# A graph layer's hot-edge counts stored column first, then source block, instead of block first

## The chip, the cores and the metric

One core of a Trainium2 chip runs the whole layer. The metric is the device time of the kernel in microseconds. The trace is one profiled execution of the same program.

## What is computed

A graph layer with three attention heads on 6,250 nodes of 128 features and 100,000 edges sorted by their target `dst`, followed by a layer norm. Cut to what matters:

```python
a_k  = exp(relu(concat(h[src], h[dst]) @ W_att_k + b_att_k))           # k = 1, 2, 3, one number per edge
att_k = segment_sum(a_k, dst)
msg  = relu(relu(relu(h[src] @ W_msg_1 + b) @ W_msg_2 + b) @ W_msg_3 + b)
m    = (a_1/att_1[dst] + a_2/att_2[dst] + a_3/att_3[dst]) / 3 * msg
out  = relu(concat(h, segment_sum(m, dst)/max(deg, 1)) @ W_c1 + b) @ W_c2 + b
x    = layernorm(x + out)
```

The message and the two halves of the attention logit depend on a node alone, so they are computed once per node. The targets are drawn unevenly: the low node numbers receive many more edges than the high ones.

## The kernel before

**Table.** A first phase computes for every node its message row and its three logits and stores them in DRAM as `message_table`. Nodes are cut into 49 blocks of 128.

**Edges by gather.** Edges are taken in groups of 256, two tiles of 128. For groups 94 to 390 (297 of them) GpSimd fetches the 128 message rows of each tile with one indirect DMA (L1154), 594 in all, into a ring of eight places of four tiles. Units are walked in order, one unit per step of all engines' loops: unit 0 has two groups, units 1 to 23 have four and take two places of the ring, units 24 to 125 have two and take one. GpSimd may fill a place once TensorE's sums of the unit that used it before are done (`s_sum`); for unit 86 that is unit 78, for unit 23 it is unit 19. In each step VectorE sums the parts of the target's logit (L1634), adds the logit of the gathered rows (L1638), waits for ScalarE's exponential (L1404), clips it (L1646) and makes weights (L1651). TensorE multiplies rows by weights (L1281) and sums the weights (L1285), and VectorE adds the result to `acc` (L1668). L1592 makes one-hot vectors for units to come.

**Hot edges by counting.** The first 94 groups point at the first 384 nodes. Their edges are not gathered but counted. A group's targets lie in a window of `w` nodes (6, 9 or 10 by the place of the group). For each edge, a number in `comb_t` joins the source's block number and the target's place in the window; targets outside the window get 4096 added so that they match nothing. VectorE turns it into a one-hot row of 49 `w` columns by comparison with a running index (`one_hots`, L1526), ScalarE makes a one-hot row of the source's place within its block (L1418, L1423), and TensorE multiplies both (L1302): the result, in a PSUM bank, is the number of edges for each place, block and column of the window. VectorE adds it to `counts` at the window's start (`add_counts`, L1539), four groups a step, in steps 1 to 24. The table `counts` holds, per partition (the source's place in its block), 49 blocks times 384 hot nodes as 16-bit integers.

**The dense product.** From step 26 on, one source block a step and 49 blocks in all: for each head ScalarE adds logits (L1374) and takes the exponential into a single PSUM bank (L1383). VectorE clips it and multiplies it by the counts of this block (`hot_weights`, L1561, three a step, 147 in all) into `hot_wt`, and TensorE multiplies `hot_wt` by the block's message rows (L1319). ScalarE may write the bank again when the weighting that reads it is done, and the weighting waits for its exponential. In a step's order on VectorE stand: head 0's weighting, L1634, L1638, L1646, L1651, head 1's weighting, L1592, head 2's weighting, L1668 twice.

After it come the final stages per group of node blocks (L836 and on, L927 and on), spread over the remaining steps, and a layer norm.

Of the kernel before, what the change touches and what calls it, by code (L numbers as in the profile page):

```python
# [45 lines left out]
CELL = 32  # L46
SUMS_AT = 64
FLT_MAX = 3.4028234663852886e38
# [42 lines left out]
def gnn_program(nc, x, x_t, src, dst, w_first, w_rest, b_rows, table, hot_table, near_table, q_table, out, n_edges):  # L91
    f32, bf16, i32 = mybir.dt.float32, mybir.dt.bfloat16, mybir.dt.int32
    ALU, ACT, AX = mybir.AluOpType, mybir.ActivationFunctionType, mybir.AxisListType.X

    n_nodes = x.shape[0]
    n_blocks = -(-n_nodes // P)
# [8 lines left out]
    n_hot = HOT_GROUPS  # L105
# [8 lines left out]
    def width_of(g):  # L114

        if g < n_hot:
            return HOT_WIDTHS[g // CELL]
        share = min(1.0, (g // CELL + 1) * CELL / n_groups)
        mean = 2 * GROUP * n_nodes / n_edges * share
        return min(WIN, 4 * -(-int(mean + 12 * share + 2 + 3.99) // 4))  # L120
# [17 lines left out]
    def block_nodes(i):  # L138
        return min(P, n_nodes - i * P)
# [5 lines left out]
    with ctx:  # L145
        def sb(name, shape, dt=f32):
            return ctx.enter_context(nc.sbuf_tensor(name, shape, dt))

        def sem(name):
            return ctx.enter_context(nc.semaphore(name))  # L150


        counts_flat = sb("counts", [P, hot_nodes * n_blocks], u16)
        counts = counts_flat[:, :].rearrange("p (b d) -> p b d", b=n_blocks)
        logits_or_x = sb("logits_or_x", [P, max(HEADS * hot_nodes, TWO * COLS)])
        hot_ld = logits_or_x[:, 0:HEADS * hot_nodes].rearrange("p (k d) -> p k d", k=HEADS)
        x_cols = logits_or_x[:, 0:TWO * COLS].rearrange("p (j n) -> p j n", j=TWO)
# [61 lines left out]
        comb_t = fin[:, at_index:at_index + n_hot * TILES].rearrange("p (g h) -> p g h", h=TILES)  # L219
# [21 lines left out]
        dst_t = sb("dst_t", [P, n_hot, TILES], bf16)  # L241
# [115 lines left out]
        def chained(eng, s):  # L357

            count = [0]

            def chain(instruction):
                count[0] += 1
                instruction.then_inc(s, 1)
                eng.wait_ge(s, count[0])
            return chain
# [239 lines left out]
        LEFT_BANK = COUNT_BANKS[LEFT_NEXT % FOUR]  # L605
        hot_end = HOT_AT + n_blocks + 2
        HOT_ADDED = 3
        INDEX_STEPS = 5 + len(range(0, n_hot, CELL))
        edges = [0, CELL, SUMS_AT, n_hot]
        assert HOT_WIDTHS[0] <= HOT_WIDTHS[1] <= HOT_WIDTHS[2] and SUMS_AT == 2 * CELL  # L610
        tally_parts = [(slice(0, n_hot), d) for d in range(HOT_WIDTHS[0])]
# [98 lines left out]
        s_cadd = sem("s_cadd")  # L710
# [5 lines left out]
        s_hw = sem("s_hw")  # L716
# [300 lines left out]
        def edge_pass(first):  # L1017
# [123 lines left out]
            with Straight(nc) if first else nc.Block() as block:  # L1141
# [221 lines left out]
                def _(act):  # L1363
# [42 lines left out]
                    def low_hots(step):  # L1406

                        if step == 0:
                            act.wait_ge(s_ix, INDEX_STEPS)
                            act.wait_ge(s_nt1, 16)  # L1410
# [63 lines left out]
                def _(dve):  # L1474
# [23 lines left out]
                    if first:  # L1498
                        index = chained(dve, s_ix)
                        scratch = hit[:, 0:2, 0:n_hot * TILES].bitcast(i32)  # L1500
                        low, high = (scratch[:, j, :].rearrange("p (h g) -> p h g", h=TILES) for j in range(2))
                        beyond = hit[:, 2, 0:n_hot * TILES].rearrange("p (g h) -> p g h", h=TILES)
                        of_src = src_t[:, :, 0:n_hot]
                        dve.wait_ge(s_src, 16)
                        index(dve.tensor_scalar(low, of_src, P - 1, None, ALU.bitwise_and))
                        index(dve.tensor_scalar(high, of_src, 7, None, ALU.logical_shift_right))
                        index(dve.tensor_copy(lo_t[:, :, :], low.rearrange("p h g -> p g h")))
                        index(dve.tensor_copy(comb_t[:, :, :], high.rearrange("p h g -> p g h")))
                        for g in range(0, n_hot, CELL):
                            cell, w = slice(g, min(g + CELL, n_hot)), float(width_of(g))  # L1510
                            dve.tensor_scalar(beyond[:, cell, :], dst_t[:, cell, :], w, BEYOND, ALU.is_ge, ALU.mult)
                            index(dve.scalar_tensor_tensor(comb_t[:, cell, :], comb_t[:, cell, :], w,
                                                           dst_t[:, cell, :], ALU.mult, ALU.add))
                        index(dve.tensor_tensor(comb_t[:, :, :], comb_t[:, :, :], beyond, ALU.add))

                    hot_window = window_registers(dve, n_hot, lambda g: hot_nodes - width_of(g))
# [12 lines left out]
                    def add_counts(step):  # L1529
                        if step == 0:  # L1530
                            dve.wait_ge(s_zero, zeroed)
                        for g in range(step * PAIRS, min((step + 1) * PAIRS, n_hot)):
                            w = width_of(g)
                            start = hot_window(g)
                            dve.wait_ge(s_ct, (g + 1) * TILES)
                            if g >= 1:
                                dve.wait_ge(s_cadd, g)
                            here = counts[:, :, bass.ds(start, w)]
                            dve.tensor_tensor(here, here, bank[COUNT_BANKS[g % FOUR]][:, 0:w * n_blocks].rearrange(  # L1539
                                "p (b d) -> p b d", d=w), ALU.add).then_inc(s_cadd, 1)  # L1540

                    def tally_hot():

# [12 lines left out]
                    def hot_weights(b, k):  # L1556
                        m, n = block_nodes(b), HEADS * b + k
                        dve.wait_ge(s_he, n + 1)
                        if b >= THREE:
                            dve.wait_ge(s_hm, b - THREE + 1)  # L1560
                        dve.scalar_tensor_tensor(hot_wt[0:m, b % THREE, k, :], bank[EXP_BANK][0:m, 0:hot_nodes],  # L1561
                                                 FLT_MAX, counts[0:m, b, :], ALU.min, ALU.mult).then_inc(s_hw, 1)

                    def copy_hot():

# [110 lines left out]
                    for i in range(n_steps):  # L1676
                        hot_step = first and 0 <= i - HOT_AT - 1 < n_blocks
                        if hot_step:
                            hot_weights(i - HOT_AT - 1, 0)
                        if i + 1 < n_units:  # L1680
                            logits_of(i + 1)
                        if first and 0 <= i - 1 < COUNT_STEPS:
                            add_counts(i - 1)
# [4 lines left out]
                        if hot_step:  # L1688
                            hot_weights(i - HOT_AT - 1, 1)
                        if i + AHEAD < n_units and by_dve(i + AHEAD):  # L1690
                            one_hot(i + AHEAD)
                        if hot_step:
                            hot_weights(i - HOT_AT - 1, 2)
# [129 lines left out]
```

## Time and profile before

| what | value |
|---|---|
| time, median of 3 runs (lowest, highest) | 826.16 us (826.0, 827.2) |
| the profiled execution, its own time | 826.97 us |
| its span, first to last instruction | 822.9 us |
| mean granted TensorE clock | 0.809 of full |
| GpSimd busy | 590.9 us, 72% |
| TensorE matmul busy | 656.1 us, 80% |
| VectorE busy | 577.4 us, 70% |
| ScalarE busy | 381.7 us, 46% |

Busy is time in which an instruction of the engine ran; issuing and waiting don't count. The span leaves out some 4 us around the first and last instruction. PE is TensorE, DVE VectorE, ACT ScalarE, POOL GpSimd.

### The profile page before, as it was taken

To read this page: it belongs to the slowest core of one execution; us is meant where nothing else is said; L and a number is where in the kernel's file an instruction comes from. 1 tells how busy PE (TensorE), PEld (TensorE's weight loads), DVE (VectorE), ACT (ScalarE), POOL (GpSimd) and SP (SyncE) were. 2 spreads that over 40 slices of the span, in tenths; PEclk is the share of its full clock that TensorE was granted. 3 is DMA by queue.
4 is the path that set the end of the run, shared out by engine and by line. 5 is a ranking of instruction groups with operands and counts; after the bars stand their busy time and mean duration, and the time that the engine had idled before them with its cause. 6 is when DMAs were issued, how large, how long until landed. Compare 5 with 4: busy or idle time off the path is not lost.

```text
span 822.9 us, 16893 instructions
## 1 busy us (share of the span) xinstructions
PE 656.1 (80%) x4917; PEld 512.9 (62%) x4917; DVE 577.4 (70%) x1934; ACT 381.7 (46%) x999; POOL 590.9 (72%) x638
## 2 busy tenths in 40 slices
PE   9945677777578778989898988888877978878885
PEld 5734455544345446778787877776666766667664
DVE  4882656585688877677776767775577868787766
ACT  5522555463444443677676767662123322333323
POOL 7437777777777777777777777777777777777770
PEclk9975555567565675799999999999699989998989
DMA  6533222225652233333333333334233443443421
GB/s 190 142 105 69 63 65 65 65 65 57 71 65 62 62 92 78 74 87 76 80 82 75 83 78 84 77 77 131 65 90 102 112 108 102 104 130 101 98 58 35
DMA packets 79474, 70.44 MB, mean 86 GB/s; under 512 B 34040, under 2 KB 65312, under 8 KB 79376
## 3 DMA queue, kind: packets, MB, share of 16 engines
q0 software_dynamic: 19008, 39.88, 22.2%
q1 hardware_dynamic: 60080, 29.28, 13.3%
q8 instruction: 42, 0.69, 0.3%
q14 instruction: 56, 0.46, 0.2%
q10 hardware_dynamic: 288, 0.13, 0.1%
HBM read 62.32 MB, written 6.90 MB: 84 GB/s over the span
## 4 chain that ended last, share of the span: by engine, by line
POOL 35%; DVE 21%; issue 19%; PE 17%; ACT 4%; DMA 2%; DVEq 2%; ACTq 0%; SPq 0%; POOLq 0%
POOL work L1154 34%; DVE fin L1561 4%; PE bank L1281 4%; DVE acc L1668 3%; ACT bank L1383 3%; DVE counts L1539 2%; DVE fin L1526 2%; DVE fin L927 2%; PE bank L836 2%; PE bank L565 2%; PE bank L544 2%; DMA work<-message_table,src_t 1%; PE bank L1285 1%; PE bank L1319 1%; DVE side L1592 1%
## 5 line engine op out<-in xcount | busy, mean ns | idle before, releaser
L1154 POOL DMA_INDIRECT work<-message_table,src_t x594 | 566.4, 953 | 191.8 <-issue 178.0
L1281 PE MATMUL bank<-work 128*128 128x144 f32 (+8 forms) x1188 | 248.7, 343 | 66.5 <-DVE acc L1668 66.4
L1281 PEld LDWEIGHTS bank<-work 128*128 128x128 f32 x1188 | 197.7, 234 | 100.4 <-issue 86.0
L1444 ACT COPY work<-bank 128x192 f32<-128x192 f32 (+7 forms) x126 | 37.4, 297 | 250.9 <-DVE work L1634 246.5
L1319 PE MATMUL bank<-work,fin 128*128 128x129 f32 (+1 forms) x882 | 117.3, 290 | 0.0
L1668 DVE TENSOR_TENSOR acc<-acc,bank 128x192 f32 (+8 forms) x297 | 88.7, 299 | 31.3 <-issue 7.5
L1319 PEld LDWEIGHTS bank<-work,fin 128*128 128x128 f32 (+1 forms) x882 | 108.2, 201 | 2.5 <-issue 0.6
L1383 ACT ACTIVATE bank<-hot_logit 128x384 f32<-128x384 f32 (+1 forms) x147 | 72.7, 494 | 70.9 <-DVE fin L1561 62.0
L1651 DVE TENSOR_TENSOR work<-bank,work 128x576 f32<-128x576 f32 (+7 forms) x126 | 86.2, 684 | 13.1
L1285 PE MATMUL bank<-work 128*4 128x48 f32 (+8 forms) x1188 | 95.0, 207 | 0.0
L1561 DVE SCALAR_TENSOR_TENSOR fin<-bank,counts 128x384 f32<-128x384 f32 (+1 forms) x147 | 81.4, 554 | 18.1 <-ACT bank L1383 17.4
L1302 PE MATMUL bank<-fin 128*128 128x294 bf16 (+2 forms) x188 | 63.7, 506 | 35.6 <-DVE fin L1526 20.4
L1374 ACT ACTIVATE hot_logit<-logits_or_x,work 128x384 f32<-128x384 f32 (+1 forms) x147 | 88.3, 600 | 0.0
L1638 DVE TENSOR_TENSOR work<-work 128x12 f32<-128x12 f32 (+1 forms) x126 | 22.2, 176 | 80.5 <-DMA work<-message_table,src_t 70.6
L836 PE MATMUL bank<-rest_w,acc 128*128 128x128 f32 x294 | 48.0, 324 | 34.2 <-DVE fin L927 29.3
L1285 PEld LDWEIGHTS bank<-work 128*4 128x4 f32 x1188 | 50.0, 88 | 38.3 <-issue 8.5
L1539 DVE TENSOR_TENSOR counts<-counts,bank 128x294 f32 (+2 forms) x94 | 57.4, 611 | 22.4 <-DVE counts L1539 12.8
L836 PEld LDWEIGHTS bank<-rest_w,acc 128*128 128x128 f32 x294 | 42.4, 227 | 36.5 <-DVE fin L927 30.6
L1302 PEld LDWEIGHTS bank<-fin 128*128 128x128 bf16 x188 | 22.5, 125 | 63.6 <-ACT fin L1423 30.7
L1418 ACT ACTIVATE fin<-fin 128x128 bf16<-128x128 f16 x188 | 59.3, 386 | 1.2 <-PE bank L1302 1.2
L1404 ACT ACTIVATE work<-work 128x12 f32<-128x12 f32 (+1 forms) x126 | 26.8, 213 | 65.4 <-DVE work L1638 63.7
L1646 DVE TENSOR_SCALAR work<-work 128x12 f32<-128x12 f32 (+1 forms) x126 | 24.5, 194 | 41.7 <-ACT work L1404 40.4
(132 smaller groups left out, 688.9 us busy)
## 6 DMA issues: line engine op xcount, KB each, us to landing
work<-message_table,src_t POOLq DMA_INDIRECT x594
side<-near_nodes SPq DMA_DIRECT2D x102, 48.0 KB
side<-logit_parts SPq DMA_DIRECT2D x297, 0.8 KB
message_table<-work SPq DMA_DIRECT2D x12, 262.0 KB, 3.4
work<-message_table SPq DMA_DIRECT2D x48, 65.5 KB
work<-in_x_t SPq DMA_DIRECT2D x12, 256.0 KB, 3.3
fin<-in_x SPq DMA_DIRECT2D x11, 256.0 KB, 2.9
logits_or_x<-in_x_t SPq DMA_DIRECT2D x11, 256.0 KB
```

Of the source, the lines that this page charges most:

```text
L836: last = pe.matmul(to[:, k * P:(k + 1) * P], acc[:, k, nodes], wc1[:, 1, :], start=True, stop=True)
L1154: pool.indirect_dma_start(out=rows_of(n)[:, t, :], out_offset=None, in_=table[:, :], in_offset=bass.IndirectOffsetOnAxis(ap=src_t[:, h, g: ...
L1281: pe.matmul(sums[:, at:at + HEADS * w], rows_here[:, t, 0:P], wt_of(i)[:, t, :], start=h == 0, stop=h == TILES - 1)
L1285: last = pe.matmul(sums[SUMS_AT:SUMS_AT + HEADS + 1, at + HEADS * w:at + HEADS * w + w], a_col[:, i % THREE, t, :], mask_of(i)[:, t, :], s ...
L1302: pe.matmul(bank[COUNT_BANKS[g % FOUR]][:, 0:n], hot_lo[:, t % HOT_RING, :], hot_comb[:, t % HOT_RING, 0:n], start=h == 0, stop=h == TILES ...
L1319: last = pe.matmul(bank[SIDE_BANKS[h]][:, k * (P + 1):(k + 1) * (P + 1)], hot_wt[0:m, b % THREE, k, h * P:(h + 1) * P], rows_here, start=F ...
L1374: act.activation(hot_logit[0:m, n % TWO, :], hot_ld[0:m, k, :], ACT.Relu, bias=hot_block[0:m, b % BLOCKS, 1 + P + k:2 + P + k]).then_inc(s ...
L1383: act.activation(bank[EXP_BANK][0:m, 0:hot_nodes], hot_logit[0:m, n % TWO, :], ACT.Exp).then_inc(s_he, 1)
L1539: dve.tensor_tensor(here, here, bank[COUNT_BANKS[g % FOUR]][:, 0:w * n_blocks].rearrange("p (b d) -> p b d", d=w), ALU.add).then_inc(s_cad ...
L1561: dve.scalar_tensor_tensor(hot_wt[0:m, b % THREE, k, :], bank[EXP_BANK][0:m, 0:hot_nodes], FLT_MAX, counts[0:m, b, :], ALU.min, ALU.mult). ...
L1651: dve.tensor_tensor(wt_of(i).rearrange("p t (k w) -> p t k w", w=w), from_q(i)[:, :, PARTS:PARTS + w].unsqueeze(2).to_broadcast([P, n, HEA ...
L1668: dve.tensor_tensor(here, here, sums[:, at:at + (HEADS + 1) * w].rearrange("p (k w) -> p k w", w=w), ALU.add).then_inc(s_acc, 1)
```

## The change

The table of counts and the columns of a group's product change their order from block first, then node, to node first, then block. The addition's operand becomes one run of 49 `w` elements of `counts`, since all blocks of one node now lie side by side. The dense product's weighting reads one block's 384 counts at a step of 49 elements. The joined number becomes 49 times the place in the window plus the block number, so that one multiply-add over all groups takes the place of three by width. The comparison with the window's width stays.

```diff
-        counts = counts_flat[:, :].rearrange("p (b d) -> p b d", b=n_blocks)
+        counts = counts_flat[:, :].rearrange("p (d b) -> p d b", b=n_blocks)
...
-        INDEX_STEPS = 5 + len(range(0, n_hot, CELL))
+        INDEX_STEPS = 6
...
                             dve.tensor_scalar(beyond[:, cell, :], dst_t[:, cell, :], w, BEYOND, ALU.is_ge, ALU.mult)
-                            index(dve.scalar_tensor_tensor(comb_t[:, cell, :], comb_t[:, cell, :], w,
-                                                           dst_t[:, cell, :], ALU.mult, ALU.add))
+                        index(dve.scalar_tensor_tensor(comb_t[:, :, :], dst_t[:, :, :], float(n_blocks),
+                                                       comb_t[:, :, :], ALU.mult, ALU.add))
                         index(dve.tensor_tensor(comb_t[:, :, :], comb_t[:, :, :], beyond, ALU.add))
...
-                            here = counts[:, :, bass.ds(start, w)]
+                            here = counts[:, bass.ds(start, w), :]
                             dve.tensor_tensor(here, here, bank[COUNT_BANKS[g % FOUR]][:, 0:w * n_blocks].rearrange(
-                                "p (b d) -> p b d", d=w), ALU.add).then_inc(s_cadd, 1)
+                                "p (d b) -> p d b", d=w), ALU.add).then_inc(s_cadd, 1)
...
                         dve.scalar_tensor_tensor(hot_wt[0:m, b % THREE, k, :], bank[EXP_BANK][0:m, 0:hot_nodes],
-                                                 FLT_MAX, counts[0:m, b, :], ALU.min, ALU.mult).then_inc(s_hw, 1)
+                                                 FLT_MAX, counts[0:m, :, b], ALU.min, ALU.mult).then_inc(s_hw, 1)
```

## Rows read from the trace of the kernel before

**Rows 1.** The page's costliest groups: busy us, mean ns, idle before, releaser.

```profile
L1154 POOL DMA_INDIRECT work<-message_table,src_t x594 | 566.4, 953 | 191.8 <-issue 178.0
```

**Rows 2.** View of L1154 (ns min/median/max, first and last start), then GpSimd's waits.

```profile
L1154 POOL DMA_INDIRECT work<-message_table,src_t x594: 940/944/1833, 54.2 to 800.4; - x198
...
POOL work L1154 <- PE bank L1285: 2.4, 8, 0.3
```

**Rows 3.** Timeline of two places of the ring: start us, us, instruction, idle before.

```profile
275.56 0.35 PE L1285 MATMUL bank<-work 128*4 128x28 f32 x4
...
281.87 0.95 POOL L1154 DMA_INDIRECT work<-message_table,src_t  x1 [0.30 <-issue]
...
580.00 0.35 PE L1285 MATMUL bank<-work 128*4 128x44 f32 x4
...
602.32 0.94 POOL L1154 DMA_INDIRECT work<-message_table,src_t  x1 [0.30 <-PE bank L1285]
```

**Rows 4.** Timeline, TensorE's last sums of units 29, 58 and 77.

```profile
341.01 0.28 PE L1285 MATMUL bank<-work 128*4 128x32 f32 x4
...
475.37 0.31 PE L1285 MATMUL bank<-work 128*4 128x40 f32 x4
...
569.13 0.32 PE L1285 MATMUL bank<-work 128*4 128x44 f32 x4
```

**Rows 5.** Timeline of VectorE, one step of the dense product.

```profile
396.95 0.56 DVE L1561 SCALAR_TENSOR_TENSOR fin<-bank,counts 128x384 f32<-128x384 f32 x1
...
398.44 0.17 DVE L1646 TENSOR_SCALAR work<-work 128x12 f32<-128x12 f32 x1 [0.55 <-ACT work L1404]
398.72 0.61 DVE L1651 TENSOR_TENSOR work<-bank,work 128x432 f32<-128x432 f32 x1
399.24 0.55 DVE L1561 SCALAR_TENSOR_TENSOR fin<-bank,counts 128x384 f32<-128x384 f32 x1
...
400.41 0.56 DVE L1561 SCALAR_TENSOR_TENSOR fin<-bank,counts 128x384 f32<-128x384 f32 x1 [0.37 <-ACT bank L1383]
400.89 0.70 DVE L1668 TENSOR_TENSOR acc<-acc,bank 128x128 f32 x2
401.59 0.56 DVE L1561 SCALAR_TENSOR_TENSOR fin<-bank,counts 128x384 f32<-128x384 f32 x1
```

**Rows 6.** View of L1638 in 341 to 570 us, then 565 to 823: idle us, times.

```profile
  DMA work<-message_table,src_t: 4.6, 6
...
  DMA work<-message_table,src_t: 22.0, 14
```

**Rows 7.** VectorE's groups by shape: busy us, mean ns, idle before.

```profile
L1561 DVE SCALAR_TENSOR_TENSOR fin<-bank,counts 128x384 f32<-128x384 f32 x144 | 79.8, 554 | 17.7 <-ACT bank L1383 17.1 <-PE bank L1319 0.4
...
L1539 DVE TENSOR_TENSOR counts<-counts,bank 128x490 f32 x30 | 20.6, 686 | 7.8 <-DVE counts L1539 3.8 <-issue 2.9 <-PE bank L1302 0.9
...
L1539 DVE TENSOR_TENSOR counts<-counts,bank 128x441 f32 x32 | 20.1, 627 | 7.2 <-DVE counts L1539 4.2 <-issue 2.9
...
L1539 DVE TENSOR_TENSOR counts<-counts,bank 128x294 f32 x32 | 16.8, 524 | 7.4 <-DVE counts L1539 4.8 <-issue 2.5
```

**Rows 8.** View of L1539 (ns min/median/max), then two neighbours in its timeline.

```profile
L1539 DVE TENSOR_TENSOR counts<-counts,bank x94: 460/617/815, 83.6 to 316.5; 128x294 f32 x32, 128x441 f32 x32, 128x490 f32 x30
...
113.09 0.46 DVE L1539 TENSOR_TENSOR counts<-counts,bank 128x294 f32 x1 [0.20 <-DVE counts L1539]
113.75 0.60 DVE L1539 TENSOR_TENSOR counts<-counts,bank 128x294 f32 x1 [0.20 <-DVE counts L1539]
```

**Rows 9.** Timeline of VectorE, three of the index preparations.

```profile
55.46 0.26 DVE L1505 TENSOR_SCALAR logits_or_x<-src_t 128x188 int32<-128x188 int32 x1
...
56.04 0.26 DVE L1507 CAST fin<-logits_or_x 128x188 f32<-128x188 int32 x1
...
57.92 0.35 DVE L1514 TENSOR_TENSOR fin<-fin,logits_or_x 128x188 f32<-128x188 f32 x1
```

**Rows 10.** Stretches: us, PE, PEld, DVE, ACT, POOL busy, clock, DMA share, GB/s.

```profile
250.00:320.00 70.00, 53.05 (x323) 33.36 (x324) 58.05 (x162) 27.51 (x78) 52.94 (x57) 0.62 0.29 73
345.00:475.70 130.70, 118.35 (x1072) 104.69 (x1069) 92.95 (x276) 93.03 (x222) 98.80 (x105) 0.96 0.34 81
```

## The prediction

> **What bounds the kernel now.** I read the costliest groups first. One group stands out: GpSimd issues 594 indirect gathers of message rows (L1154), each 0.95 us, and nearly all of its 191.8 us of idle time between them is issue time [rows 1]. The line's own view gives the first at 54.2 us and the last at 800.4 us: (800.4 - 54.2) / 593 = 1.258 us each, and in the list of waits the only other releaser inside that stream is the edge sums of TensorE (L1285), 2.4 us in 8 pieces of at most 0.3 us, no longer than the issue gap itself [rows 2]. So from 54 us to 800 us GpSimd never stops. The span is 54.2 + 746.2 + a tail of 22.5 us behind the last gather's start, and nothing that VectorE saves in between can move the end; only what makes GpSimd wait, or leaves VectorE and TensorE with a backlog behind the last gather, can.
>
> GpSimd may run eight ring places ahead of the edge sums. I read from the timeline how near it came to that limit. In the counting stage the place for the gathers starting at 281.87 us was free when the sum of four long units before had ended at 275.56 + 0.35 = 275.91: 6.0 us of slack, the least of the whole run. The gather at 602.32 us is the 437th, the first of unit 86; it needs the sum of unit 78, which ended at 580.00 + 0.35: 22.0 us of slack [rows 3]. Unit 78 is the first behind the dense product, whose 49 blocks ride on steps 27 to 76.
>
> In the dense stage the edge sums of unit 29 end at 341.29, those of unit 58 at 475.68, and those of unit 77 at 569.45 us [rows 4]: 228.2 us for 48 steps, 4.75 us a step, against 4 x 1.258 = 5.03 us for a unit's gathers. The stage is a little faster than the gathers and eats backlog. What sets a step is seen in VectorE's timeline, one step from 396.95 to 401.59 us [rows 5]. All three weightings (L1561) stand in VectorE's order; idle are 0.55 us for ScalarE's exponential of the edges and 0.37 us for the next hot exponential in PSUM (one bank, so ScalarE waits for each weighting in turn). Those idle times follow from ScalarE's own work behind the previous weighting and don't shrink if a weighting grows. So a weighting longer by x lengthens the step by 3x.
>
> How much of such a delay is swallowed? VectorE's first addition that needs gathered rows (L1638) waited for the gather DMA 4.6 us in the dense stage and 22.0 us from there to the end [rows 6]. A consumer that is late doesn't wait there. So 26.6 us of lateness disappear. The ring says the same in another way: after 4.6 us swallowed in the stage, 22.0 us of slack before GpSimd must stop.
>
> **The change part by part.** (1) Addition of counts, 94 times. It took 524, 627 and 686 ns as means of its three widths, 57.5 us in all [rows 7]. Its minimum is 460 ns, and neighbours of the same 294 elements took 0.46 and 0.60 us [rows 8]; what differs is the node at which the window starts, hence where the 49 short runs of 12 bytes lie. I take the one-run form at the good value of each width: 460 for 294 elements, and by VectorE's slope of (554 - 460) / (384 - 294) = 1.04 ns per element [rows 7, 8] 613 for 441 and 664 for 490. Saved: 32 x 64 + 32 x 14 + 30 x 22 ns = 3.2 us of VectorE. Up to about 225 us VectorE waits for gathers anyway and the slack of the ring is never used up, so this saves nothing at the end; of the wider groups some 0.8 us reach the start of the dense stage as less backlog. If the window start multiplied by 49 needs one more register step of some tens of ns each, this vanishes too.
>
> (2) Indices. Three chained multiply-adds become one over 188 elements; the addition behind it has that size and took 0.35 us [rows 9]. That stands near 57 us, before the first gathered rows are used, and the gain of some 0.4 us is hidden by the gathers. Comparisons, one-hots, matmuls and their sizes are unchanged: a group's 49 w columns are only in another order.
>
> (3) The dense product's weighting, 147 times, now reads its 384 counts at a step of 49 elements, 98 bytes, instead of as one run. Today 554 ns [rows 7]. This is the price that decides, and no row shows this very access. Lower bound: L1507 reads int32 at a step of 376 bytes and took 0.26 us, as L1505 does over the same 188 elements read in a row [rows 9], so x = 0. But that instruction alternates between two runs, so each neighbour comes back two elements later, while a step of 98 bytes never comes back. Upper bound: a badly placed window of 49 short runs costs 0.60 - 0.46 = 0.14 us more, 2.9 ns per jump [rows 8]; 384 jumps would be x = 1.1 us. Nearer to the new access is the mean over placements, since 98-byte steps run through all of them: 524 - 460 = 64 ns for 49 jumps, 1.3 ns per jump, read and write together [rows 7, 8]. If the read alone pays all of it, x = 384 x 1.3 = 0.50 us; if it pays half, 0.25 us. I take 0.40 us, about one more cycle per element by the slope above, so a weighting of 0.95 us. A rule of the Trainium skill speaks against this change: "Vector Engine (DVE) Microarchitecture Reference", section "Measured stream behaviour on trn2", holds that a port keeps its rate only over adjacent pairs of words, and gives 1.73 ns an element for a source that hops every time and 2.50 ns for steps of 24 words, against 1.054 ns. By it, as an estimate, x would be 0.26 or 0.56 us, on both sides of mine; no row of this trace shows such a step, and by the row of L1507 alone x would be nothing.
>
> (4) The sum. Lateness made: 49 x 3 x 0.40 = 58.8 us, less 0.8 us from (1). Swallowed: 26.6 us. Left: 58.8 - 0.8 - 26.6 = +31.4 us. GpSimd's issue is then stretched by the same 31 us, mostly between about 400 and 650 us, when the ring is full. In general the end moves by 147 x - 27.4 us once x is over 0.186 us, and not at all below. The profiled execution took 826.97 us at a span of 822.9; the median of the runs is 826.16. 826.16 + 31.4 = 857.6 us; I say 857.5.
>
> **Rivals.** What a measurement of this kernel can tell from no change is 0.2%, 1.7 us.
>
> A, the forecast, weighting between 0.85 and 1.15 us: +17 to +60 us. Chance 0.47.
>
> B, a mild price, x between 0.19 and 0.30 us: +1 to +17 us; 0.25 gives +9.4, 835.5 us. For it: half of the mean jump price, and a source in PSUM that may hide part. Chance 0.20, of which 0.02 lies within 0.2%.
>
> C, the other side: the strided read is free or nearly so. The place is the read in L1561, the point is x = 0.186 us. GpSimd stays unbroken and the time is 826.2 us; the 3.2 us of the additions show on VectorE and nowhere at the end. For it: L1507, and most windows whose runs jump 768 bytes at no price; against it: those runs still hold 6 or more elements per jump. Chance 0.18, including 0.03 for a gain over 0.2% by less contention at the tail.
>
> D, heavier: x over 0.60 us (at the upper bound 147 x 1.1 - 27.4 = +134 us), or TensorE's clock falls in the dense stage. It was granted 0.62 in 250 to 320 us and 0.96 in 345 to 475.7 us, where TensorE was busy 118.35 of 130.7 us, 4.2 us a step [rows 10]; at a step of 5.95 us it would be busy 71%. At half clock its work would be at most 8.1 us a step (4.23 x 0.96 / 0.5), longer than VectorE's, and the end 49 x (8.1 - 4.65) - 27 = +142 us if it held for the whole stage. Against it: from 345 us on it kept the upper of its two levels, 2.4 GHz, nearly all the time, at shares of 80% and more. Chance 0.15.
>
> So slower by over 0.2%: 0.47 + 0.18 + 0.15 = 0.80; within 0.2%: 0.02 + 0.15 = 0.17; faster 0.03. The range has to include C and nearly all of A: 825 to 885 us (x from 0 to 0.58). It leaves out D and little else.
>
> **What the profile of the changed kernel would show.** L1561 near 0.95 us instead of 0.55; the addition at L1539 near 460, 613 and 664 ns with hardly any spread; steps in the dense stage of about 5.9 us; waits of GpSimd's L1154 for TensorE's L1285 of some 30 us, from the middle of the dense stage on; L1638 hardly waiting for gathers after it; the first gather still at 54 us and the tail behind the last one near 22 us. The prediction is wrong if L1561 stays under 0.74 us, if ScalarE's exponentials turn out to leave slack that hides part of 3x, or if the clock falls.

## The result and the profile after

The changed kernel takes 867.16 us (median of 4 runs, 864.21 to 869.08) against 826.46 us for the one before (4 runs): 40.7 us more. The ratio on record is 1.0508, interval 1.0490 to 1.0526; it is formed from the single runs and not from these two medians, whose own ratio is 1.0492. The profiled execution took 866.57 us at a span of 862.5 us, 39.6 us more than the span of before.

VectorE's groups by shape in the changed kernel (busy us, mean ns, idle before), the lines that answer to [rows 7]:

```profile
L1561 DVE SCALAR_TENSOR_TENSOR fin<-bank,counts 128x384 f32<-128x384 f32 x144 | 140.8, 978 | 16.9 <-ACT bank L1383 16.9
...
L1539 DVE TENSOR_TENSOR counts<-counts,bank 128x490 f32 x30 | 20.0, 667 | 8.6 <-DVE counts L1539 4.8 <-issue 2.6 <-PE bank L1302 0.9
L1539 DVE TENSOR_TENSOR counts<-counts,bank 128x441 f32 x32 | 19.7, 616 | 8.0 <-DVE counts L1539 4.8 <-issue 3.0
```

The weighting went from 554 to 978 ns, so x is 0.424 us, and 147 of them make 62.3 us. The additions took what one run should: 667 and 616 ns here, and the view of the line gives the minimum as before and the maximum down from 815 to 671 ns. In sum they fell from 57.4 to 54.5 us:

```profile
L1539 DVEq FUSED_REGOPS  x94: 57/64/71, 83.3 to 317.0; - x94
L1539 DVE TENSOR_TENSOR counts<-counts,bank x94: 460/615/671, 83.5 to 317.1; 128x294 f32 x32, 128x441 f32 x32, 128x490 f32 x30
```

The register step in front of each addition now takes 64 ns at the median; it was 46. The idle time of VectorE before the additions grew from 22.4 to 24.4 us over all 94, so VectorE gained 0.9 us and not 2.9.

One step on VectorE's timeline, answering to [rows 5]:

```profile
396.72 0.98 DVE L1561 SCALAR_TENSOR_TENSOR fin<-bank,counts 128x384 f32<-128x384 f32 x1
...
398.62 0.22 DVE L1646 TENSOR_SCALAR work<-work 128x12 f32<-128x12 f32 x1 [0.54 <-PE bank L1285]
398.94 0.56 DVE L1651 TENSOR_TENSOR work<-bank,work 128x384 f32<-128x384 f32 x1
399.42 0.97 DVE L1561 SCALAR_TENSOR_TENSOR fin<-bank,counts 128x384 f32<-128x384 f32 x1
...
401.01 0.98 DVE L1561 SCALAR_TENSOR_TENSOR fin<-bank,counts 128x384 f32<-128x384 f32 x1 [0.36 <-ACT bank L1383]
401.91 0.70 DVE L1668 TENSOR_TENSOR acc<-acc,bank 128x128 f32 x2
402.61 0.98 DVE L1561 SCALAR_TENSOR_TENSOR fin<-bank,counts 128x384 f32<-128x384 f32 x1
```

The step lasts 5.89 us, 1.25 more than the 4.64 of before, which is 3 x 0.42; the two idle pieces are the same (0.54 and 0.36 against 0.55 and 0.37). The profile puts this 0.54 us down to TensorE's L1285; most of the waits before L1646, 36.5 of 43.4 us on the page, it puts down to ScalarE's L1404 as before. Over the whole stage the steps grew by 1.24 us: 287.5 / 48 = 5.99 us against 4.75. TensorE's last sums of units 29 and 77, and of the last unit, 125:

```profile
341.96 0.28 PE L1285 MATMUL bank<-work 128*4 128x32 f32 x4
...
629.42 0.32 PE L1285 MATMUL bank<-work 128*4 128x44 f32 x4
...
847.86 0.33 PE L1285 MATMUL bank<-work 128*4 128x48 f32 x4
```

Against [rows 4] unit 29 is 0.9 us later, unit 77 60.3 us later (629.74 - 569.45), the last one (808.77 us before) 39.4 us later. So the delay is made in the dense stage, and a third of it vanishes behind it. (Some 2 us of the 60.3 arise at unit 77 itself, by a lower clock there; see "3x per step" below.) GpSimd's own view and its waits, answering to [rows 2]:

```profile
L1154 POOL DMA_INDIRECT work<-message_table,src_t x594: 938/944/1754, 54.3 to 832.9; - x198
```

```profile
POOL work L1154 <- issue: 166.5, 546, 0.4
POOL work L1154 <- PE bank L1285: 48.8, 45, 2.8
```

It is held 45 times, 48.8 us with the issue gaps of 0.3 us in them, some 35 us without. The first time shows on its timeline at 441.79 us, and from there to 636 us the ring is full:

```profile
441.79 0.94 POOL L1154 DMA_INDIRECT work<-message_table,src_t  x1 [1.01 <-PE bank L1285]
...
636.07 0.94 POOL L1154 DMA_INDIRECT work<-message_table,src_t  x1 [1.36 <-PE bank L1285]
```

The second row is unit 86's first gather, 33.8 us later than in [rows 3]; it is the last one that is held. The last gather starts at 832.9 us, 29.6 us before the end of the span, where it was 22.5 us. From the dense stage on L1638 no longer waits for gathers: in 341 us to the end its views show no such wait, where [rows 6] had 4.6 and 22.0 us.

### The profile page after: what moved, and what is told of

It reads as the page before. It is cut to its first block, busy times and chain, and to the rows that moved or that the text cites. A ratio compares the mean times of both kernels' runs of the same rounds, so it can differ in the third digit from the quotient of the medians.

```text
span 862.5 us, 16891 instructions
## 1 busy us (share of the span) xinstructions
PE 665.2 (77%) x4917; PEld 521.0 (60%) x4917; DVE 637.5 (74%) x1932; ACT 381.4 (44%) x999; POOL 588.2 (68%) x638
## 3 DMA queue, kind: packets, MB, share of 16 engines
q1 hardware_dynamic: 60080, 29.28, 12.7%
## 4 chain that ended last, share of the span: by engine, by line
DVE 36%; issue 18%; PE 18%; POOL 15%; ACT 8%; DVEq 2%; DMA 2%; ACTq 0%; SPq 0%; POOLq 0%
POOL work L1154 15%; DVE fin L1561 14%; PE bank L1281 5%; ACT bank L1383 5%; DVE acc L1668 4%; DVE counts L1539 2%; DVE fin L927 2%; PE bank L836 2%; DVE fin L1526 2%; DVE work L1646 2%; PE bank L1285 2%; DVE side L1592 2%; PE bank L544 2%; DVE work L1651 1%; PE bank L565 1%
## 5 line engine op out<-in xcount | busy, mean ns | idle before, releaser
L1154 POOL DMA_INDIRECT work<-message_table,src_t x594 | 563.7, 949 | 226.8 <-issue 166.5
L1281 PEld LDWEIGHTS bank<-work 128*128 128x128 f32 x1188 | 195.5, 232 | 139.7 <-issue 126.5
L1561 DVE SCALAR_TENSOR_TENSOR fin<-bank,counts 128x384 f32<-128x384 f32 (+1 forms) x147 | 143.8, 978 | 17.3 <-ACT bank L1383 17.2
L1444 ACT COPY work<-bank 128x192 f32<-128x192 f32 (+7 forms) x126 | 37.4, 297 | 247.7 <-DVE work L1634 246.8
L1319 PE MATMUL bank<-work,fin 128*128 128x129 f32 (+1 forms) x882 | 129.4, 309 | 0.0
L1319 PEld LDWEIGHTS bank<-work,fin 128*128 128x128 f32 (+1 forms) x882 | 119.8, 219 | 2.4 <-issue 0.2
L1285 PE MATMUL bank<-work 128*4 128x48 f32 (+8 forms) x1188 | 94.9, 207 | 0.0
L1302 PE MATMUL bank<-fin 128*128 128x294 bf16 (+2 forms) x188 | 64.5, 513 | 37.4 <-DVE fin L1526 26.6
L1285 PEld LDWEIGHTS bank<-work 128*4 128x4 f32 x1188 | 49.9, 88 | 38.0 <-issue 8.2
L1539 DVE TENSOR_TENSOR counts<-counts,bank 128x294 f32 (+2 forms) x94 | 54.5, 580 | 24.4 <-DVE counts L1539 14.8
L836 PE MATMUL bank<-rest_w,acc 128*128 128x128 f32 x294 | 46.1, 315 | 26.2 <-DVE fin L927 25.4
L1638 DVE TENSOR_TENSOR work<-work 128x12 f32<-128x12 f32 (+1 forms) x126 | 21.9, 174 | 58.6 <-DMA work<-message_table,src_t 46.4
L1302 PEld LDWEIGHTS bank<-fin 128*128 128x128 bf16 x188 | 22.5, 128 | 66.3 <-ACT fin L1423 34.9
L1418 ACT ACTIVATE fin<-fin 128x128 bf16<-128x128 f16 x188 | 59.3, 386 | 1.2 <-PE bank L1302 1.2
L836 PEld LDWEIGHTS bank<-rest_w,acc 128*128 128x128 f32 x294 | 40.8, 220 | 28.4 <-DVE fin L927 26.6
L1646 DVE TENSOR_SCALAR work<-work 128x12 f32<-128x12 f32 (+1 forms) x126 | 24.0, 191 | 43.4 <-ACT work L1404 36.5
L1592 DVE TENSOR_SCALAR side<-side,less_col 48x512 bf16<-48x512 bf16 x149 | 52.6, 366 | 0.0
```

What stands on the lines that cost most here:

```text
L836: last = pe.matmul(to[:, k * P:(k + 1) * P], acc[:, k, nodes], wc1[:, 1, :], start=True, stop=True)
L1154: pool.indirect_dma_start(out=rows_of(n)[:, t, :], out_offset=None, in_=table[:, :], in_offset=bass.IndirectOffsetOnAxis(ap=src_t[:, h, g: ...
L1281: pe.matmul(sums[:, at:at + HEADS * w], rows_here[:, t, 0:P], wt_of(i)[:, t, :], start=h == 0, stop=h == TILES - 1)
L1285: last = pe.matmul(sums[SUMS_AT:SUMS_AT + HEADS + 1, at + HEADS * w:at + HEADS * w + w], a_col[:, i % THREE, t, :], mask_of(i)[:, t, :], s ...
L1302: pe.matmul(bank[COUNT_BANKS[g % FOUR]][:, 0:n], hot_lo[:, t % HOT_RING, :], hot_comb[:, t % HOT_RING, 0:n], start=h == 0, stop=h == TILES ...
L1319: last = pe.matmul(bank[SIDE_BANKS[h]][:, k * (P + 1):(k + 1) * (P + 1)], hot_wt[0:m, b % THREE, k, h * P:(h + 1) * P], rows_here, start=F ...
```

## Experiments

**Which part of the change makes the time.** The changed kernel with a contiguous read:

```diff
-                                                 FLT_MAX, counts[0:m, :, b], ALU.min, ALU.mult).then_inc(s_hw, 1)
+                                                 FLT_MAX, counts_flat[0:m, b * hot_nodes:(b + 1) * hot_nodes], ALU.min, ALU.mult).then_inc(s_hw, 1)
```

> The changed kernel, but the weighting reads 384 counts in one run (the counts it reads belong to other nodes and blocks, so the dense product is not the layer's). Theory, the strided read alone sets the change: L1561 back at 554 ns, GpSimd issues without a stop from 54 to 800 us, time 826.5 us, within 1.7. The additions stay at 460, 615 and 667 ns and their 3 us do not show at the end. Rival 1, the rest of the change (longer register step of 57 to 71 ns in place of 46 before each of 94 additions, other index arithmetic) costs what my sum missed: 829 to 832 us. Rival 2, the faster additions reach the end: 823 to 824.5 us.

Measured: 826.91 us against 826.62 before, ratio 1.0006 (0.9996 to 1.0015). Its shapes:

```profile
L1561 DVE SCALAR_TENSOR_TENSOR fin<-bank,counts 128x384 f32<-128x384 f32 x144 | 79.8, 554 | 17.3 <-ACT bank L1383 17.3
...
L1539 DVE TENSOR_TENSOR counts<-counts,bank 128x294 f32 x32 | 14.8, 463 | 7.9 <-DVE counts L1539 5.1 <-issue 2.6
```

The faster additions (463 ns in place of 524 for the narrow groups), with their longer register step, and the single index step are worth nothing at the end. Both rivals fall.

The other half, the kernel before with the strided read alone:

```diff
+        by_node = counts_flat[:, :].rearrange("p (d b) -> p d b", b=n_blocks)
...
-                                                 FLT_MAX, counts[0:m, b, :], ALU.min, ALU.mult).then_inc(s_hw, 1)
+                                                 FLT_MAX, by_node[0:m, :, b], ALU.min, ALU.mult).then_inc(s_hw, 1)
```

> The kernel before, its additions and indices as they were; only the weighting reads at a step of 49 elements (the counts it reads belong to other nodes and blocks, so the dense product is not the layer's). Theory: L1561 near 978 ns, step of the dense stage 5.9 to 6.0 us, GpSimd held by the edge sums for 30 to 35 us, time 864 to 869 us as for the whole change. Rival 1, of the 40.7 us some 5 come from the rest of the change: 860 to 863 us.

Measured: 866.56 us, ratio 1.0474 (1.0440 to 1.0509). The view of the line (one number later here, for the added line):

```profile
L1562 DVE SCALAR_TENSOR_TENSOR fin<-bank,counts x147: 953/978/1017, 326.4 to 619.1; 128x384 f32<-128x384 f32 x144, 106x384 f32<-106x384 f32 x3
```

The strided read alone loses 39.9 us (36 to 42 by the interval), against 40.7 for the whole change; the rival of 860 to 863 us falls, narrowly. GpSimd was held 48.8 us in 41 pieces, some 36.5 without issue gaps, a little over the 30 to 35 expected. One kernel with everything but the strided read loses nothing, the other with the strided read alone loses all: this pair settles the cause.

**Is a first part of the lateness free?** The same kernel with `by_node[0:m, :, b] if k < 1 else counts[0:m, b, :]`, so that only head 0 reads at a step:

> The kernel before, but head 0's weighting alone (one of three in each step) reads at a step of 49 elements; that head's hot sums are not the layer's. Theory, lateness is made at 49 x 0.424 = 20.8 us and the first 22 to 27 us are swallowed (waits for gathers that fall away, slack of the ring): time 826.5 to 828 us, L1154 never held by L1285 for more than its issue gap. Rival, each strided weighting costs the end its share, 40.7 / 3: 840 us.

Measured: 829.74 us (10 runs, 825.75 to 833.78), ratio 1.0034 (1.0016 to 1.0052), so 3 us and not 13.6: the proportional rival falls, and the theory's 826.5 to 828 was a little low. GpSimd, as expected, is not held at all, neither by its starts nor by its waits, which are ordinary issue gaps:

```profile
L1155 POOL DMA_INDIRECT work<-message_table,src_t x594: 940/944/1761, 54.3 to 798.5; - x198
...
POOL work L1155 <- PE bank L1286: 2.7, 9, 0.3
```

Its last gather starts no later than in the kernel before (800.4 us), and this execution, 831.98 us, is 5 us longer all the same. So the end can move without GpSimd ever being held.

With `k < 2`, two heads:

> The kernel before, but heads 0 and 1 (two weightings of three in each step) read at a step of 49 elements; these heads' hot sums are not the layer's. Theory: 98 x 0.424 = 41.6 us of lateness less 22 to 27: 841 to 846 us, L1154 held by L1285 for 12 to 18 us. Rival, a share of two thirds: 853.6 us.

Measured: 851.77 us (5 runs, 845.39 to 853.27), ratio 1.0319 (1.0302 to 1.0336), 25.2 us more. Above the theory's range, and the interval (some 851.6 to 854.4 us) holds the rival's 853.6: by the time alone the rival would stand here. What speaks against it is the kernel with one head, and the profiled execution, which was the fastest one, 845.39 us, inside the theory's range; GpSimd was held there 20.8 us in 23 pieces, 14 without issue gaps, as the theory had it. To see where the others lose, further executions with their profile:

> The same kernel as two_heads_strided, another execution with its profile. The profiled one there took 845.4 us, where the sum gives 845, and the timed ones 850 to 853. Theory: the sum holds for the profiled one and the others lose some 7 us in another place; an execution near 852 shows it either as longer dense steps than 5.58 us, at a lower granted TensorE clock, or as more than 218 us from the sums of unit 77 to those of unit 125. Rival: none reaches 850 with a profile, and the place stays open.

> As two_heads_b, a third execution: 845 or 850 to 853 us, with the difference in the same place.

> The same kernel as one_head_strided, another execution; its timed ones lay between 825.8 and 833.8 us. Theory: the end is the later of GpSimd's last gather plus 22 us and the sums of unit 77 plus 219 and 14 us, so it is 826 us if the sums of unit 77 come by 588 us, and later by as much as they do.

They took 845.32, 851.85 and 826.93 us. The ends of the sums (L1285, here L1286) from the timelines, in us, with the differences that matter:

| kernel | unit 29 | unit 77 | unit 125 | 29 to 77 | 77 to 125 | time of this execution |
|---|---|---|---|---|---|---|
| before | 341.3 | 569.5 | 808.8 | 228.2 | 239.3 | 826.97 |
| one_head_b | 340.0 | 587.7 | 809.1 | 247.7 | 221.4 | 826.93 |
| one_head_strided | 342.1 | 592.1 | 813.5 | 250.0 | 221.4 | 831.98 |
| two_heads_b | 340.3 | 610.9 | 827.3 | 270.6 | 216.4 | 845.32 |
| two_heads_strided | 341.4 | 609.4 | 827.6 | 268.0 | 218.2 | 845.39 |
| two_heads_c | 342.6 | 613.0 | 833.6 | 270.4 | 220.6 | 851.85 |
| the changed kernel | 342.2 | 629.7 | 848.2 | 287.5 | 218.5 | 866.57 |
| only_strided | 344.0 | 631.6 | 851.5 | 287.5 | 219.9 | 869.62 |

What the reader is to see stands in the last but one column. Paced by the gathers, the stage behind unit 77 takes 239.3 us. Once it is late enough never to wait for a gather, it takes 216 to 221 us whatever the lateness: that is its own pace, and the difference, 18 to 23 us, is what can be made up. The two executions with one head show it too: in neither does L1639, the L1638 of before, wait for a gather behind 341 us, and the one whose sums of unit 77 come 4.4 us later takes 5.0 us longer. The rule forecast for one_head_b (sums of unit 77 plus 219 and 14 us, plus 4 for what the span leaves out) gives 825 and 829 us, 2 to 3 us too little.

The execution at 851.85 us came to unit 29 2.3 us later than that at 845.32 us, to unit 77 2.1 us later, and lost 4.2 us more behind it. So two thirds of the 6.5 us are lost behind unit 77, a third ahead of unit 29, and none in the dense steps (270.4 against 270.6 us); the rival that no execution reaches 850 us with a profile falls. Their stretches (us, PE, PEld, DVE, ACT, POOL busy, clock, DMA share, GB/s), first of two_heads_b:

```profile
600.00:700.00 100.00, 85.89 (x704) 69.31 (x704) 77.58 (x279) 27.21 (x92) 72.15 (x76) 0.91 0.41 106
700.00:820.00 120.00, 100.02 (x833) 80.31 (x832) 95.87 (x352) 36.99 (x121) 88.06 (x92) 0.96 0.40 102
```

and of two_heads_c:

```profile
600.00:700.00 100.00, 84.03 (x686) 67.87 (x685) 76.35 (x273) 25.44 (x87) 70.86 (x76) 0.89 0.40 105
700.00:820.00 120.00, 104.01 (x798) 84.25 (x797) 93.01 (x335) 38.02 (x123) 88.84 (x94) 0.88 0.40 101
```

The slower one was granted 0.88 where the faster had 0.96 and did fewer matmuls (798 against 833) in more busy time. That is one pair of executions. The ten timed ones of one_head_strided order the same way: the four with a mean clock of 0.817 and more took 825.8 to 828.3 us, the six with 0.814 and less 829.7 to 833.8. But one_head_b took 826.93 us at 0.802, and the four of the changed kernel do not order by it. That the clock causes the spread is likely and not shown. The kernel before spreads over 2.1 us in 19 runs and over 4.2 in the 10 of another chip, those with one and two heads over 8: as long as the gathers set the pace, such differences seem to be hidden.

**What a strided read costs.** The kernel before, each block's weightings reading in another pattern, by a function of the block:

```diff
+                    STEPS = (1, 2, 3, 4, 5, 6, 7, 8, 9, 12, 16, 24, 32, 48, 49)
+
+                    def stepped(m, b, k):
+                        flat = counts_flat[0:m, :]
+                        s = b % 20
+                        if s < 15:
+                            n = hot_nodes * STEPS[s]
+                            return flat[:, 0:n].rearrange("p (d b) -> p d b", b=STEPS[s])[:, :, STEPS[s] - 1 if k == 1 else 0]
+                        if s < 19:
+                            j = (2, 4, 8, 16)[s - 15]
+                            v = flat.rearrange("p (d b j) -> p d b j", b=n_blocks, j=j)
+                            return v[:, :, b % n_blocks, :]
...
```

> The kernel before, but block b's three weightings read their 384 counts in another pattern each: steps of 1, 2, 3, 4, 5, 6, 7, 8, 9, 12, 16, 24, 32, 48, 49 elements for b mod 20 = 0 to 14, runs of 2, 4, 8, 16 elements with a hop behind each for 15 to 18, and a step of 24 four-byte elements for 19 (the counts read are other ones, so the dense product is not the layer's; the whole is one look for the duration of each instruction). Theory, what costs is each access that leaves a 16-byte line: 554 ns up to a step of 2 to 4 elements, rising from there to 978 ns at 8 and more and flat from there on; runs of 4 and more elements cost nothing. Rival 1, anything but unit step costs the full 424 ns. Rival 2, the price depends on the width of the hop, 48 other than 49 and 32, by a conflict of addresses; the four-byte step of 24 (96 bytes) shows whether the 2-byte element matters.

Three weightings a block, two or three blocks a pattern. From its timeline, one instruction of a pattern each: step 4, 5, 6, 7, 8, then 48 and 49, then runs of 2, and four-byte elements at a step of 24:

```profile
339.68 0.56 DVE L1581 SCALAR_TENSOR_TENSOR fin<-bank,counts 128x384 f32<-128x384 f32 x1
...
345.12 0.60 DVE L1581 SCALAR_TENSOR_TENSOR fin<-bank,counts 128x384 f32<-128x384 f32 x1
...
349.78 0.70 DVE L1581 SCALAR_TENSOR_TENSOR fin<-bank,counts 128x384 f32<-128x384 f32 x1
...
354.79 0.76 DVE L1581 SCALAR_TENSOR_TENSOR fin<-bank,counts 128x384 f32<-128x384 f32 x1
...
359.98 0.85 DVE L1581 SCALAR_TENSOR_TENSOR fin<-bank,counts 128x384 f32<-128x384 f32 x1
...
393.34 1.11 DVE L1581 SCALAR_TENSOR_TENSOR fin<-bank,counts 128x384 f32<-128x384 f32 x1
...
399.56 0.98 DVE L1581 SCALAR_TENSOR_TENSOR fin<-bank,counts 128x384 f32<-128x384 f32 x1
...
405.47 0.56 DVE L1581 SCALAR_TENSOR_TENSOR fin<-bank,counts 128x384 f32<-128x384 f32 x1
...
425.09 1.10 DVE L1581 SCALAR_TENSOR_TENSOR fin<-bank,counts 128x384 f32<-128x384 f32 x1
```

| pattern, 384 elements of 2 bytes | ns, all instructions of it |
|---|---|
| steps 1 to 4 (2 to 8 bytes) | 546 to 559 |
| step 5 / 6 / 7 | 567 to 597 / 659 to 704 / 748 to 767 |
| steps 8, 9, 12, 16, 24 (16 to 48 bytes) | 815 to 867 |
| step 32 (64 bytes) | 786 to 807 |
| step 48 (96 bytes) | 1095 to 1108 |
| step 49 (98 bytes) | 966 to 984 |
| runs of 2, 4, 8, 16 with a hop of 49 runs | 548 to 559 |
| step 24 of 4-byte elements (96 bytes) | 1097 to 1110 |

The theory's form holds up to 48 bytes: free while two elements or more come from 16 bytes, then a price per 16 bytes entered. Its size does not: at a step of 8 it had 978 ns, flat from there on, and 815 to 867 ns were measured up to a step of 24, and more only beyond 32. The fixed part is 554 - 384 x 1.04 = 154 ns; at a step of 16 bytes (845 - 154) / 384 = 1.80 ns per line. With it, a step of 5 enters 240 lines and gives 586 ns, a step of 6 288 lines and 672, a step of 7 336 lines and 759, all within the measured ranges. The price is fitted at one step and met at three others; that lines of 16 bytes are behind it is the reading that fits, and no other run tests it. Rival 1 falls. Rival 2 is right in part: beyond 48 bytes the distance matters, 64 bytes the cheapest and 96 the dearest, and the element's width does not (1.10 us for 2 and for 4 bytes). The weighting at 98 bytes pays (980 - 154) / 384 = 2.15 ns an element. Why 96 and 98 bytes cost more than 48 or 64 stays open. The whole of this kernel took 836.4 us in its one run, 11.5 us more than the kernel before on that chip (824.91), for 24.2 us of added weighting: here only 12.7 us of lateness disappeared.

The Trainium skill says of SBUF ("SBUF — State Buffer", section "Specifications (TRN2)") that its lines are of 16 bytes and want two hits each for the full rate; the steps of 8 and of 16 bytes agree. The measured table of the Trainium skill ("Vector Engine (DVE) Microarchitecture Reference", section "Measured stream behaviour on trn2") has 1.73 ns an element for one source that hops 4 KiB every time, and 2.50 to 2.51 ns for both sources, or the destination alone, at a step of 24 words, which is 96 bytes. These are not the accesses of this kernel; the prices here lie near them, 1.80 ns for one source at 16 bytes and (1104 - 154) / 384 = 2.47 ns for one source at 96 bytes. The rule of that section, runs of two adjacent 4-byte words, does not fit 2-byte elements: runs of two elements, 4 bytes, cost nothing here.

**Does GpSimd's issue set the end of the kernel before?** Two more hot groups, 590 gathers:

```diff
-HOT_GROUPS = 94
+HOT_GROUPS = 96
...
-    long_end = long_from + (LONG - 1) * 2 * pair
+    long_end = long_from + LONG * 2 * pair
...
-    first_order = [tuple(range(n_hot, long_from))]
+    first_order = []
```

> The kernel before with 96 instead of 94 hot groups, so that GpSimd issues 590 gathers in place of 594; all results as the layer's. Theory, GpSimd's issue sets the end: 4 x 1.258 = 5.0 us less, 821.4 us (820 to 823), though two more groups are counted on VectorE (4 comparisons of 0.38 us and 2 additions of 0.67 us) and the dense product stays. Rival, the counting stage's added work or the tail takes it back: 825 to 828 us.

Measured: 819.98 us against 824.91 for the kernel before on this chip, ratio 0.9944 (0.9927 to 0.9960), 4.9 us less where 5.0 were forecast. Its view of the line:

```profile
L1154 POOL DMA_INDIRECT work<-message_table,src_t x590: 940/944/1830, 54.0 to 793.5; - x197
```

Four gathers less are worth their issue time, and the work added on VectorE nothing. The edit does one thing more: the first unit of two groups is gone and one more unit has four, so there are 124 units and steps in place of 126. That fewer steps gave the gain is a rival that this run doesn't exclude; for the issue time speaks that GpSimd's stream goes on unbroken, (793.5 - 54.0) / 589 = 1.256 us each, as in the kernel before. This version, with the counts block first as before, beats both kernels. More groups were not tried: by the way the targets are drawn, the first 384 nodes receive some 24,800 edges, a little under 97 groups of 256.

## Why the prediction was right, point by point

**The bound** was right for the kernel before: 594 gathers at 1.258 us each. Taking away four of them fits it to 0.1 us, and in run_read_in_after VectorE's small gain in the additions has no effect.

**The additions** were right in size, 54.5 us against 54.3 predicted. That 0.8 us of it would reach the dense stage was not seen: the first weighting starts at 325.6 us, 0.6 later than before. The case that the prediction names for this came in, a longer register step, 64 ns in place of 46, and with it 2.0 us more of idle time before the additions. Over all executions with 94 hot groups the first weighting starts between 323.1 and 326.7 us, with additions of either kind, so terms of this size are below what one execution tells.

**The weighting** was forecast at 0.95 and measured 0.978 us. The value was chosen between two bounds, and the reason given for it, the mean price of a jump in the old additions, is not the mechanism the pattern kernel shows. That 0.40 came within 6% of 0.424 is therefore in part luck. At a step of 48 elements, one less, x would have been 1.104 - 0.554 = 0.55 us, and at 32 elements 0.25 us; nothing in the argument of bounds and jumps tells these steps apart, and by the same formula they are worth +53 and +9 us. Whether the lower row (L1507) was free because each of its 16-byte stretches comes back, as I argued, or for another reason, no run here tells.

**3x per step** was right: 1.25 us for 3 x 0.424, with the same two idle pieces. From the start of the first weighting to that of the last the stage took 236.4 us before (325.0 to 561.4) and 293.0 us now (325.6 to 618.6), 56.6 us more. The 146 weightings between make 61.9 us, so 5.3 us were swallowed in the stage, where I took 4.6. By TensorE's sums of units 29 and 77 the stage grew by 59.3 us, but unit 77 is an uneven mark: its sums stand behind the product of the last block, whose 18 matmuls (L1319) took 4.24 us at a granted clock of 0.50 in this trace and 2.28 us at 1.00 in the one before.

**What is swallowed** is the term that was mis-sized. The step was "so 26.6 us of lateness disappear". By L1638's waits 22.0 us would be made up behind the dense product. Measured were 239.3 - 218.5 = 20.8 from the sums of unit 77 on, or 247.4 - 229.6 = 17.8 from the start of the last weighting to the last sum. In all, 62.3 - 39.4 = 22.9 us disappeared. With x = 0.424 my formula gives 147 x 0.424 - 27.4 = +34.9, and +39.4 was measured on the last sums; the 4.5 us between them are 3.7 us of the swallowed part and the 0.8 us of the additions. The whole miss, 867.2 us measured against 857.5 said, is these 4.5 us, 3.5 us for x = 0.424 in place of 0.40, and 1.7 us by which the medians and the profiled executions differ. By the medians of all kernels even less disappeared than 26.6 us: 21.6 us in the changed kernel, 22.4 in only_strided, 17.7 of 20.8 with one head, 16.4 of 41.6 with two, 12.7 of 24.2 in the single run with the patterns. Why it varies is open beyond what is said of the clock above. A stage that no longer waits for gathers meets its own pace, with other waits in place of those that vanish, and wants a little more than the old time less the old waits.

**The ring** was said to give the same limit in another way. It doesn't: the last gather starts 32.5 us later (832.9 against 800.4), the last sum 39.4 us. GpSimd held is the mark of a full ring, not the cause of the end: with one head it is never held and the profiled execution is 5 us longer all the same. Behind unit 86 GpSimd isn't held any more, and the edge path on VectorE and TensorE, which waits for no gather there, sets the time. That is also where a sign of the prediction failed: the tail behind the last gather is 29.6 us and not near 22.

**Case A** came in. Of the others: C (free read) fell with L1561, B with its size. D's clock fell hardly: it was granted 0.91 in 345 to 475.7 us, against 0.96 before [rows 10]:

```profile
345.00:475.70 130.70, 100.21 (x834) 88.03 (x834) 101.70 (x218) 73.53 (x176) 95.33 (x101) 0.91 0.31 74
```

TensorE was busy 77% there, where I had reckoned 71%.

## What to carry to other kernels

When a layout is turned, one side's short runs become the other side's strided read. Count instructions and elements on both sides: 94 additions gained 2.9 us of busy time, most of it lost again in waits before them, and 147 weightings lost 62.3 us. A strided read of 2-byte elements on VectorE was free here as long as two elements came from each 16 bytes (steps up to 8 bytes, 546 to 559 ns) or from each hop (runs of two), so these are the layouts to look for. Slack measured as waits on an input that is late anyway was more than could be made up in every kernel here (26.6 us against 13 to 23); a stage's own pace behind it is found by delaying it on purpose.

## What the runs showed of the hardware that I had not expected

Steps of 96 bytes (2.47 ns an element) and of 98 bytes (2.15 ns) are dearer than 64 bytes ((800 - 154) / 384 = 1.68 ns). In the kernel before, 49 short runs were mostly free even with a hop of 768 bytes behind each: of the 94 additions those of a width had one base time (460, about 615, about 666 ns), and 26 of the 94 took some 45 or 145 ns more; with one run all of this is gone (460 to 466, 612 to 619, 665 to 671 ns). Which placements pay was not tried.
